# Adapter and expert products of an adaptive FFN kernel, done as packed products of rounded halves and remainders

## The chip, the cores and the metric

The kernel runs on one core of a Trainium2 chip. The metric is the device time of one execution in microseconds. Durations and starts below come from one profiled execution of the kernel before the change.

## What is computed

x has 8 batches of 256 tokens of 1024 features. The first layer quantizes x (8 groups of thresholds, each with its own step and zero point) and puts the result through a mixture of 4 experts of rank 16, of which the router keeps the best 2 by token. The second layer is linear in what comes out of the first: a weight W with a rank-32 adapter chosen by the batch's label, then a kernel K with a rank-32 adapter mixed by a gate, a shared rank-32 adapter and a bias; its result is added to its input.

```python
...
x = x + L0_ffn(L0_cond(x, thresholds, deltas, zero_points), router_w, A, B)
...
base = einsum('bsi,oi->bso', x, W)
low = einsum('bsi,bir->bsr', x, lora_A[labeler_index])
h = base + einsum('bsr,or->bso', low, lora_B_w) * 0.5
...
base_out = matmul(h, kernel) + bias
delta = einsum('bor,btr->bto', B_eff, einsum('bri,bti->btr', A_eff, h))
delta += einsum('or,btr->bto', lora_B_shared, einsum('ri,bti->btr', lora_A_shared, h))
...
x = x + base_out + delta
```

## The kernel before

Because the second layer is linear, the kernel first makes the combined matrix P = I + W'(K + shared adapter), 1024 x 1024, and then the result is x P + bias plus products of low rank. All work is laid out by hand on five engines with semaphores; each engine takes its instructions strictly in the order in which its function writes them, and SyncE's and GpSimd's queues issue the DMAs in order too.

A number a is kept as a rounded half a_hi and a remainder a_lo, both float32r, and a product is taken as a_hi b_hi + a_hi b_lo + a_lo b_hi: three float32r products. Where the factors are plain float32, one product shows in the trace as two records.

The quantization runs beside everything else on ScalarE and VectorE. Its work is cut into 64 groups, `quant(c, g)` for batch c and threshold group g. For one group ScalarE makes `level` (L395) and `val` (L406), and VectorE clips `val` (L598), makes the mask `inside` (L608) and merges (L615); group 1 has two masks, group 0 has the clip alone, and after group 7 VectorE closes the batch (L620). `val`, `level` and `inside` turn over a few buffers, so ScalarE may be only two groups ahead.

**The first part** (to about 202 us) has 16 steps, `for n in range(STEPS)` at each engine. Step n makes one 128 x 512 tile of P. In steps 0 to 7 TensorE first makes tile n of u, the gate's adapters put through W and the label's adapter (L896, 8 float32 products, and L898) in `ubank`; ScalarE copies it to `ust` (L537), which counts `u_made`, and SyncE stores it to `u_dram`. There are two `ust` buffers. TensorE may overwrite `ubank` once `u_made` has counted. Then come the 24 products of the tile (L913, L914, L917), and one k_update (L796). On ScalarE a step is: `weight_hi` of a later tile (L424), the copy of u, `p_out(n - 1)` (L525), the quantization groups of the table `GROUPS`. On VectorE: `k_add` (L647), `weight_lo` (L639), `p_out(n - 1)` (L745), the groups, and the expert ranking where it is due. Steps 1, 6 and 7 among others have one group, steps 2, 4 and 5 two. Between steps 7 and 8 stand `v_product(1)` (L806) and the split of the second half of K (`kp_split`, L431; `kp_lo_part`, L652).

After step 15 TensorE puts the experts' output factor through P (L933 to L935, 48 products of 128 x 512), ScalarE copies that out four times (`bp_out`, L469), and x of batch 0 is split (`x_part`, L455 and L707).

**The second part** runs over 8 batches b of 8 slots j. In a slot TensorE does 12 of the products of x and P (L965 to L967). The slots hold further work at fixed places:

- after slot 4 of each batch, `z_begin(b + 1)`: the adapters with the experts' factor, 64 x 64 (L870), and x with the adapters, 64 x 256 (L874), both plain float32 from `ub` and `xs`; ScalarE copies the first out (`bu_out`, L462);
- near slot 7, `z_end`: one product that adds the experts' share (L881), which ScalarE copies to `zt` (L571), and `close`, the products of `zt` and the adapters' rows `tb` (L942);
- `mid(c)`: the quantized batch c with the experts' A and the router (L848), which waits for VectorE's L620 of that batch. `mid(7)` stands after slot 1 of batch 7. VectorE's ranking of batch c begins with L679 and waits for it;
- the transposes L858 and the output copies L480, 3 slots or more after their tile.

x is loaded in whole batches of 1 MB into one buffer `xs`; batch b + 1 may land when `z_begin(b)` has read it and ScalarE and VectorE have split it.

## Time and profile before

| | us |
|---|---|
| median of 3 runs | 488.16 |
| lowest, highest | 486.01, 490.64 |
| profiled execution, whole | 489.24 |
| its span | 487.5 |
| TensorE busy | 471.8 |
| VectorE busy | 391.4 |
| ScalarE busy | 356.6 |

The span runs from the first to the last instruction; 1.74 us lie outside it. TensorE's busy time rests on modelled ends of pipelined products, so an engine that reads as busy isn't at its peak, and the distance between starts tells more than a record's duration. In timelines the idle time before an instruction stands in brackets with what released it.

### The profile page before, as it was taken

Reading aid. Unit: us, or ns where it says so; the run is one execution under the profiler, and the core shown is the slowest. Engines: PE = TensorE matmul, PEld = TensorE weight load, DVE = VectorE, ACT = ScalarE, POOL = GpSimd, SP = SyncE. Lnnn points to the kernel's source line nnn. Section 1 sums busy time; section 2 is a strip of 40 time slices with the busy share of each in tenths; the row PEclk is TensorE's granted clock in tenths of the full one; section 3 lists DMA queues with packets and bytes.
Section 4 is the critical chain, followed back from the end, with each engine's and each line's share of the span. In section 5 each row is a group of like instructions: output and inputs, shape, how many; then the busy total and the mean of one; then the engine's idle time right before and its main releaser. Section 6 shows DMA issues by size and latency. Waiting matters only on the chain.

```text
span 487.5 us, 5645 instructions
## 1 busy us (share of the span) xinstructions
PE 471.8 (97%) x2200; PEld 365.7 (75%) x2200; DVE 391.4 (80%) x381; ACT 356.6 (73%) x297; POOL 6.8 (1%) x12
## 2 busy tenths in 40 slices
PE   6989999999889999999999999999999999999896
PEld 5963788887648888787777777787787768767774
DVE  3289978789979989939879989798799994999400
ACT  3779987864978398676699599776899697776001
POOL 0000000001000001000000000000000000000000
PEclk9599999999999999999999999999999999999799
DMA  8975542313301527030441316014214013102002
GB/s 281 422 267 178 171 142 73 90 43 98 107 0 37 181 86 204 13 108 1 151 141 44 108 54 200 38 55 130 108 54 152 0 55 129 56 0 86 1 0 87
DMA packets 35500, 50.61 MB, mean 104 GB/s; under 512 B 26610, under 2 KB 26866, under 8 KB 33074
## 3 DMA queue, kind: packets, MB, share of 16 engines
q1 hardware_dynamic: 34322, 41.87, 26.7%
q0 software_dynamic: 1152, 8.39, 4.8%
q8 instruction: 17, 0.28, 0.2%
q14 instruction: 9, 0.07, 0.1%
HBM read 39.51 MB, written 10.49 MB: 103 GB/s over the span
## 4 chain that ended last, share of the span: by engine, by line
PE 76%; DVE 16%; issue 4%; DMA 2%; ACT 1%; SPq 0%; DVEq 0%; ACTq 0%
PE bank L965 10%; PE bank L966 10%; PE bank L967 10%; DVE val L615 7%; PE bank L848 6%; PE bank L942 5%; PE bank L874 5%; PE bank L917 5%; PE bank L913 5%; PE bank L914 4%; PE bank L896 3%; DVE inside L608 3%; PE bank L814 3%; DVE val L598 2%; DMA la<-la_in 2%
## 5 line engine op out<-in xcount | busy, mean ns | idle before, releaser
L406 ACT ACTIVATE val<-level,shift,small 128x2048 f32<-128x2048 int16 x64 | 133.8, 2091 | 16.3 <-DVE val L615 16.2
L615 DVE COPY_PREDICATED val<-inside,val 128x2048 f32<-128x2048 uint8 x56 | 141.3, 2523 | 0.3
L395 ACT ACTIVATE level<-xq,inv 128x2048 int16<-128x2048 f32 x64 | 127.9, 1998 | 2.0 <-DMA xq<-xt_in 1.4
L598 DVE TENSOR_SCALAR val<-val,width,unshift 128x2048 f32<-128x2048 f32 x64 | 86.0, 1347 | 22.7 <-ACT val L406 22.4
L965 PE MATMUL bank<-p_hi,x_hi 128*128 128x512 f32 x256 | 102.5, 401 | 0.0
L966 PE MATMUL bank<-p_lo,x_hi 128*128 128x512 f32 x256 | 100.4, 392 | 0.0
L967 PE MATMUL bank<-p_hi,x_lo 128*128 128x512 f32 x256 | 100.4, 392 | 0.0
L608 DVE TENSOR_SCALAR inside<-absx,thr 128x2048 uint8<-128x2048 f32 x56 | 71.4, 1285 | 7.1 <-ACT absx L387 7.1
L965 PEld LDWEIGHTS bank<-p_hi,x_hi 128*128 128x128 f32 x256 | 48.5, 189 | 17.6 <-issue 8.8
L966 PEld LDWEIGHTS bank<-p_lo,x_hi 128*128 128x128 f32 x256 | 48.4, 189 | 10.5 <-issue 0.5
L967 PEld LDWEIGHTS bank<-p_hi,x_lo 128*128 128x128 f32 x256 | 48.3, 189 | 10.5
L913 PE MATMUL bank<-kp_hi,w_hi 128*128 128x512 f32 x128 | 50.8, 397 | 1.8 <-DVE kp_lo L652 1.8
L917 PE MATMUL bank<-kp_hi,w_lo 128*128 128x512 f32 x128 | 50.4, 393 | 0.0
L914 PE MATMUL bank<-kp_lo,w_hi 128*128 128x512 f32 x128 | 49.9, 390 | 0.0
L848 PEld LDWEIGHTS bank<-ra,val 128*128 128x128 f32 x256 | 31.5, 202 | 3.0 <-DVE val L620 1.7
L848 PE MATMUL bank<-ra,val 128*128 128x68 f32 x256 | 31.5, 284 | 1.3 <-DVE val L620 1.3
L942 PE MATMUL bank<-tb,zt 128*128 128x512 f32 x64 | 32.7, 599 | 0.0
L896 PE MATMUL bank<-aefft,wst 128*128 128x256 f32 x128 | 29.1, 380 | 2.2 <-ACT ust L537 2.2
L874 PE MATMUL bank<-xs,ub 128*64 128x256 f32 x128 | 29.3, 382 | 0.0
L896 PEld LDWEIGHTS bank<-aefft,wst 128*128 128x128 f32 x128 | 24.1, 190 | 6.9 <-issue 3.4
L913 PEld LDWEIGHTS bank<-kp_hi,w_hi 128*128 128x128 f32 x128 | 24.1, 188 | 6.3 <-issue 2.0
L917 PEld LDWEIGHTS bank<-kp_hi,w_lo 128*128 128x128 f32 x128 | 24.0, 188 | 5.2
(91 smaller groups left out, 477.4 us busy)
## 6 DMA issues: line engine op xcount, KB each, us to landing
xq<-xt_in POOLq DMA_DIRECT2D x8, 1024.0 KB, 5.8
xs<-xt_in SPq DMA_DIRECT2D x8, 1024.0 KB, 4.9
out_t<-ost SPq DMA_DIRECT2D x16, 512.0 KB, 3.0
wst<-w_in SPq DMA_DIRECT2D x14, 512.0 KB, 3.6
la<-la_in SPq DMA_DIRECT2D x4, 512.0 KB, 10.4
kst<-k_in SPq DMA_DIRECT2D x4, 512.0 KB, 13.9
lb<-lb_in SPq DMA_DIRECT2D x1, 2048.0 KB, 18.7
kst<-k_in SPq DMA_DIRECT2D x1, 2048.0 KB, 7.9
```

Source lines behind the costliest of these rows:

```text
L395: nc.scalar.activation(level[:, g % 2], xq[:, c % 2], ACT.Copy, scale=inv[:, g:g + 1]).then_inc(levels_made, 1)
L406: nc.scalar.activation(val[:, turn(c, g)], level[:, g % 2], ACT.Relu, bias=shift[:, g:g + 1], scale=par[:, 1, g:g + 1]).then_inc(raised, 1)
L598: nc.vector.tensor_scalar(v, v, width[:, g:g + 1], unshift[:, g:g + 1], ALU.min, ALU.add).then_inc(valued, 1)
L608: nc.vector.tensor_scalar(inside[:, g % 2], absx, thr[:, g - 1:g], None, ALU.is_le).then_inc(masked, 1)
L615: nc.vector.copy_predicated(val[:, acc(c)], inside[:, g % 2], val[:, turn(c, g)]).then_inc(merged, 1)
L848: last = mm(midbank[:, t * RT:(t + 1) * RT], val[:, acc(c), k, t * P:(t + 1) * P], ra[:, k], start=k == 0, stop=k == KT - 1)
L913: mm(obank[n % RING], w_hi[side(n)][:, o], kp_hi[:, o], start=o == 0, stop=False)
L914: mm(obank[n % RING], w_hi[side(n)][:, o], kp_lo[:, o], start=False, stop=False)
L917: last = mm(obank[n % RING], w_lo[side(n)][:, o], kp_hi[:, o], start=False, stop=o == KT - 1)
L965: mm(o, x_hi[:, s, k, at], p_hi[:, h, k], start=False, stop=False)
L966: mm(o, x_hi[:, s, k, at], p_lo[:, h, k], start=False, stop=False)
L967: last = mm(o, x_lo[:, s, k, at], p_hi[:, h, k], start=False, stop=False)
```

## The change

Three products are done in another form.

- The experts' factor is no longer split twice over 128 columns that hold it twice. `betp` holds the remainder in columns 0 to 63 and the rounded half in columns 64 to 127. Its product with P takes two products in place of three (`betp` with p_hi and with p_lo); the two halves of the result lie in different partitions of the bank. ScalarE copies the lower to `tb` (`bp_lo_out`), VectorE adds the upper (`bp_add`), and one copy on ScalarE makes the second `tb` (`bp_copy`).
- The adapters are kept as halves and remainders, 128 columns `packed` (half u, half label adapter, remainder u, remainder label adapter). u is split when it is made: ScalarE writes `ust[:, :, 0]`, VectorE `ust[:, :, 1]` (`u_lo`), and `u_made` is now counted by `u_lo`. There is one `ust` buffer, so ScalarE waits for the store of the tile before. The label adapters of all 5 labels are loaded once (0.66 MB), split (`al_hi` on ScalarE, `al_lo` on VectorE) and stored to `al_dram` (1.3 MB), from where `adapters(b)` loads them.
- `z_begin` is cut in two. `bu_begin(b + 1)` comes after slot 4, 8 products of 128 x 128. ScalarE and VectorE then sum its parts (`bu_out`, `bu_add`). `z_begin(b + 1)` comes after slot 5: 16 float32r products of 128 x 256, `packed` with x_hi and x_lo. It waits for `bu_made` and for both halves of x_lo. ScalarE and VectorE sum its two halves (`z_lo_out`, `z_add`), and `z_end` multiplies all 128 rows of `zt` with `bu`, whose first 64 rows hold the identity.

x is staged in halves of 512 KB (`xs_half`), since z no longer reads `xs`; batch 0's second half has a buffer of its own (`xs_last`). ScalarE splits x after slots 0 and 3 (before: 1 and 3). The ends of batch 0 (`ZEND`, `CLOSE`) move by two slots. Arrays change places in memory.

```diff
-    XAT, ZAT = (1, 3), 4
+    XAT, BUAT, ZAT = (0, 3), 4, 5
...
+            sp.wait_ge(afull, KT // 2)
+            sp.dma_start(al_raw, a["al"].rearrange("l p k r -> p l k r")).then_inc(al_in, 16)
...
+            sp.wait_ge(al_made, 1)
+            sp.dma_start(al_dram.rearrange("l p k h r -> p l (k h r)"),
+                         al_hl.rearrange("p l k h r -> p l (k h r)").bitcast(F32)).then_inc(al_stored, 16)
...
             def u_store(i):
+                sp.wait_ge(u_hi_made, i + 1)
                 sp.wait_ge(u_made, i + 1)
...
             def x_part(c, p):
-                act.wait_ge(xs_in, 16 * (c + 1))
+                if c == 0 and p:
+                    act.wait_ge(xs_last_in, 16)
+                else:
+                    act.wait_ge(xs_in, 16 * (c * XPARTS + p + (c == 0)))
...
+            def z_lo_out(c):
+
+                act.wait_ge(z_read, c + 1)
+                if c >= ZSLOTS:
+                    act.wait_ge(ofull, STEPS + (c - ZSLOTS + 1) * TILES)
+                nc.scalar.activation(zt[0:2 * R, c % ZSLOTS], zbank[2 * R:P, 0:TOK], ACT.Copy).then_inc(z_lo_made, 1)
...
             quant(*ORDER[3])
             v_rows(0)
+            al_hi()
...
                 if n < KT:
                     act.wait_ge(ufull, n + 1)
-                    if n >= 2:
-                        act.wait_ge(u_stored[n % 2], 16 * (n // 2))
-                    nc.scalar.activation(ust[:, n % 2], ubank, ACT.Copy).then_inc(u_made, 1)
+                    if n:
+                        act.wait_ge(u_stored, 16 * n)
+                    nc.scalar.activation(ust[:, :, 0], ubank.rearrange("p (b r) -> p b r", b=BATCH), ACT.Copy).then_inc(u_hi_made, 1)
...
+            def u_lo(n):
+                dve.wait_ge(u_hi_made, n + 1)
+                nc.vector.tensor_tensor(ust[:, :, 1], ubank.rearrange("p (b r) -> p b r", b=BATCH), ust[:, :, 0].bitcast(F32), ALU.subtract).then_inc(u_made, 1)
...
+            def z_add(c):
+
+                dve.wait_ge(z_lo_made, c + 1)
+                z = zt[0:2 * R, c % ZSLOTS]
+                nc.vector.tensor_tensor(z, zbank[0:2 * R, 0:TOK], z, ALU.add).then_inc(z_summed, 1)
+
+            def bu_add(c):
+
+                dve.wait_ge(bu_lo_made, c + 1)
+                part = bu_parts[2 * R:P]
+                nc.vector.tensor_tensor(part, zbank[2 * R:P, TOK:TOK + P], part, ALU.add).then_inc(bu_summed, 1)
+                dve.wait_ge(bu_summed, c + 1)
+                if c >= 2:
+                    dve.wait_ge(zfull, c - 1)
+                nc.vector.tensor_tensor(bu[2 * R:P, c % 2], part[:, 0:2 * R], part[:, 2 * R:4 * R], ALU.add).then_inc(bu_made, 1)
...
             quant(*ORDER[4])
+            al_lo()
...
-                for c, g in GROUPS[n]:
+                for i, (c, g) in enumerate(GROUPS[n]):
                     quant(c, g)
+                    if i == 0 and n < KT:
+                        u_lo(n)
...
+                    if b + 1 < BATCH and j - 1 == BUAT:
+                        bu_add(b + 1)
+                    if b + 1 < BATCH and j - 1 == ZAT:
+                        z_add(b + 1)
                     ranks(slot(b, j))
                     for c, g in GROUPS[slot(b, j)]:
                         quant(c, g)
...
-                    mm(sbank[h], bet_hi[:, k], p_hi[:, h, k], start=o == 0, stop=False)
-                    mm(sbank[h], bet_hi[:, k], p_lo[:, h, k], start=False, stop=False)
-                    last = mm(sbank[h], bet_lo[:, k], p_hi[:, h, k], start=False, stop=o == KT - 1)
+                    mm(sbank[h], betp[:, k], p_hi[:, h, k], start=o == 0, stop=False)
+                    last = mm(sbank[h], betp[:, k], p_lo[:, h, k], start=False, stop=o == KT - 1)
...
+            def z_begin(c):
+
+                t = c % 2
+                packed = ub[:, t].rearrange("p k h a r -> p k (h a r)")
+                pe.wait_ge(bu_made, c + 1)
+                pe.wait_ge(x_lo_made, (c + 1) * XPARTS)
                 for k in range(KT):
-                    last = mm(zbank[0:2 * R, 0:TOK], ub[:, t, k], xs[:, k], start=k == 0, stop=False)
+                    mm(zbank[:, 0:TOK], packed[:, k], x_hi[:, t, k], start=k == 0, stop=False)
+                    last = mm(zbank[:, 0:TOK], packed[:, k], x_lo[:, t, k], start=False, stop=k == KT - 1)
                 last.then_inc(z_read, 1)
```

VectorE's order in steps 0 and 1 of the first part, before (each row: line, operation, output and inputs, shape, the semaphores it waits for):

```order
L598 TENSOR_SCALAR val<-val,width,unshift 128x2048 [waits raised]
L608 TENSOR_SCALAR inside<-absx,thr 128x2048 [waits merged]
L615 COPY_PREDICATED val<-inside,val 128x2048 [waits merged,masked,valued]
L647 TENSOR_TENSOR kst<-bank,kst 128x512 [waits kfull,k2_in]
L639 TENSOR_TENSOR w_lo_100<-wst_102,w_hi_98 128x1024 [waits ofull,w_hi_made]
L745 TENSOR_TENSOR p_lo<-bank,p_hi 128x512 [waits p_hi_made]
```

And the same place with the change, from `al_lo` on:

```order
L766 TENSOR_TENSOR al_hl<-al_raw,al_hl 128x40x32 [waits al_hi_made]
L648 TENSOR_SCALAR val<-val,width,unshift 128x2048 [waits raised]
L658 TENSOR_SCALAR inside<-absx,thr 128x2048 [waits merged]
L665 COPY_PREDICATED val<-inside,val 128x2048 [waits merged,masked,valued]
L762 TENSOR_TENSOR ust<-bank,ust 128x8x32 [waits u_hi_made]
L697 TENSOR_TENSOR kst<-bank,kst 128x512 [waits kfull,k2_in]
L689 TENSOR_TENSOR w_lo_101<-wst_103,w_hi_99 128x1024 [waits ofull,w_hi_made]
L825 TENSOR_TENSOR p_lo<-bank,p_hi 128x512 [waits p_hi_made]
```

L766 and L762 are new; L762, which frees `ubank` for TensorE's next step, stands behind the step's first quantization group.

TensorE's order around z in batch 1, before:

```order
L870 MATMUL bank<-ub,bet 64x64 [waits zt_made,bu_made,bet_in,ub_in1]
L870 MATMUL bank<-ub,bet 64x64 x7
L874 MATMUL bank<-xs,ub 64x256 [waits xs_in]
L874 MATMUL bank<-xs,ub 64x256 x7
L965 MATMUL bank<-p_hi,x_hi 128x512
```

and with the change, where slot 5 and `mid(3)` (L939) come between the two:

```order
L961 MATMUL bank<-ub,betp 128x128 [waits bu_made,zt_made,ub_in0]
L961 MATMUL bank<-ub,betp 128x128 x7
L1064 MATMUL bank<-p_hi,x_hi 128x512
...
L939 MATMUL bank<-ra,val 128x68 [waits mgt_made,ra_in,q_made]
L939 MATMUL bank<-ra,val 128x68 x15
L971 MATMUL bank<-x_hi,ub 128x256 [waits x_lo_made,bu_made]
L972 MATMUL bank<-x_lo,ub 128x256
```

z moved behind slot 5, takes 16 products of 128 weight columns, and waits for two results of VectorE.

VectorE's order at the same place with the change, slots 4 to 6 of a batch; before, the groups followed L707 (here L757) directly:

```order
L757 TENSOR_TENSOR x_lo<-xs,x_hi 128x1024 [waits x_hi_made]
L783 TENSOR_TENSOR bu_parts<-bank,bu_parts 64x128 [waits bu_lo_made]
L787 TENSOR_TENSOR bu<-bu_parts 64x64 [waits zfull,bu_summed]
L648 TENSOR_SCALAR val<-val,width,unshift 128x2048 [waits raised]
L658 TENSOR_SCALAR inside<-absx,thr 128x2048 [waits merged]
L665 COPY_PREDICATED val<-inside,val 128x2048 [waits merged,masked,valued]
L777 TENSOR_TENSOR zt<-bank,zt 64x256 [waits z_lo_made]
```

Three sums are new, and through L783 and L777 VectorE waits for TensorE's two products.

## Rows read from the trace of the kernel before

**Rows 1.** The page: busy time by engine over the whole span.

```profile
PE 471.8 (97%) x2200; PEld 365.7 (75%) x2200; DVE 391.4 (80%) x381; ACT 356.6 (73%) x297; POOL 6.8 (1%) x12
```

**Rows 2.** The chain that ended last, in order of time: start us, us, what.

```profile
141.36 0.62 ACT kp_hi L431
...
142.84 0.47 PE bank L913
...
154.24 3.52 PE bank L848 x32
```

**Rows 3.** VectorE's timeline, steps 0 to 2 and the end of batch 1.

```profile
62.43 0.68 DVE L647 TENSOR_TENSOR kst<-bank,kst 128x512 f32<-128x512 f32 x1
...
64.81 0.69 DVE L745 TENSOR_TENSOR p_lo<-bank,p_hi 128x512 fp32r<-128x512 f32 x1 [0.57 <-ACT p_hi L525]
65.41 1.34 DVE L598 TENSOR_SCALAR val<-val,width,unshift 128x2048 f32<-128x2048 f32 x1
...
70.32 0.67 DVE L647 TENSOR_TENSOR kst<-bank,kst 128x512 f32<-128x512 f32 x1
...
137.16 2.35 DVE L620 SCALAR_TENSOR_TENSOR val<-absx,thr,val 128x2048 f32<-128x2048 f32 x1
```

**Rows 4.** TensorE's timeline, steps 1 and 7: start, us, line, xrecords, [idle before].

```profile
59.80 3.62 PE L896 MATMUL bank<-aefft,wst 128*128 128x256 f32 x16
...
123.82 3.69 PE L896 MATMUL bank<-aefft,wst 128*128 128x256 f32 x16 [2.23 <-ACT ust L537]
```

**Rows 5.** ScalarE's timeline, steps 0 and 1.

```profile
57.47 0.37 ACT L537 ACTIVATE ust<-bank 128x256 f32<-128x256 f32 x1
...
63.90 0.38 ACT L537 ACTIVATE ust<-bank 128x256 f32<-128x256 f32 x1 [1.24 <-PE bank L898]
64.18 0.59 ACT L525 ACTIVATE p_hi<-bank 128x512 fp32r<-128x512 f32 x1
```

**Rows 6.** VectorE's timeline, second part.

```profile
212.50 1.23 DVE L707 TENSOR_TENSOR x_lo<-xs,x_hi 128x1024 fp32r<-128x1024 f32 x1 [4.27 <-ACT x_hi L455]
...
246.66 1.35 DVE L598 TENSOR_SCALAR val<-val,width,unshift 128x2048 f32<-128x2048 f32 x1 [4.55 <-ACT val L406]
...
412.13 0.17 DVE L679 COPY lg<-bank 128x8 f32<-128x8 f32 x1 [5.84 <-PE bank L848]
...
437.64 1.23 DVE L707 TENSOR_TENSOR x_lo<-xs,x_hi 128x1024 fp32r<-128x1024 f32 x1
...
452.43 2.35 DVE L620 SCALAR_TENSOR_TENSOR val<-absx,thr,val 128x2048 f32<-128x2048 f32 x1
```

**Rows 7.** TensorE's timeline, second part.

```profile
201.47 0.39 PE L934 MATMUL bank<-p_lo,bet_hi 128*128 128x512 f32 x1
201.69 0.39 PE L935 MATMUL bank<-p_hi,bet_lo 128*128 128x512 f32 x1
...
433.04 0.97 PE L870 MATMUL bank<-ub,bet 128*64 128x64 f32 x13
...
434.06 3.40 PE L874 MATMUL bank<-xs,ub 128*64 128x256 f32 x15
...
454.84 5.71 PE L848 MATMUL bank<-ra,val 128*128 128x68 f32 x32 [1.29 <-DVE val L620]
```

**Rows 8.** Groups by form: VectorE's smallest product read from PSUM.

```profile
L701 DVE TENSOR_TENSOR mg<-bank,gates 128x128 f32<-128x128 f32 x8 | 2.3, 291 | 0.3
```

**Rows 9.** DMA issues on the page: KB each, median us to landing.

```profile
u_dram<-ust SPq DMA_DIRECT2D x8, 128.0 KB, 4.0
```

**Rows 10.** TensorE's timeline, a short float32r product between long ones.

```profile
54.44 0.22 PE L916 MATMUL bank<-ident 128*128 128x128 f32 x1
54.50 0.44 PE L917 MATMUL bank<-kp_hi,w_lo 128*128 128x512 f32 x1
54.78 0.39 PE L913 MATMUL bank<-kp_hi,w_hi 128*128 128x512 f32 x1
```

**Rows 11.** Windows of 2 us: TensorE busy, granted clock, DMA share, GB/s.

```profile
458.00:460.00 2.00, 2.00 (x11) 0.50 0.00 0
```

More of the change, by code:

```diff
@@ L134, in build @@
     w_bytes = KT * P * 4
-    w_hi = [place(f"w_hi{i}", [P, KT, P], F32R, xs_at, 2 * i * w_bytes)[0] for i in range(2)]
-    w_lo = [place(f"w_lo{i}", [P, KT, P], F32R, xs_at, (2 * i + 1) * w_bytes)[0] for i in range(2)]
-    wst = [place(f"wst{i}", [P, KT, P], F32, at)[0] for i, at in enumerate((ub_at, bet_at))]
+    w_hi = [place(f"w_hi{i}", [P, KT, P], F32R, ub_at, 2 * i * w_bytes)[0] for i in range(2)]
+    w_lo = [place(f"w_lo{i}", [P, KT, P], F32R, ub_at, (2 * i + 1) * w_bytes)[0] for i in range(2)]
+    wst = [place(f"wst{i}", [P, KT, P], F32, at)[0] for i, at in enumerate((xs_at, betp_at))]
     ident_raw, _ = place("ident_raw", [P, P], F32, zt_at)
@@ L251, in former @@
         return {KT: KT - 1, KT + 1: KT - 2}.get(m, m - 2)
-    ZEND = [max(b * KT - 1, OUT_AT[b] - STEPS) for b in range(BATCH)]
-    CLOSE = [max(b * KT + 1, ZEND[b] + 1) for b in range(BATCH)]
+    ZEND = [max(b * KT - 1, OUT_AT[b] - STEPS, 1) for b in range(BATCH)]
+    CLOSE = [max(b * KT + 1, ZEND[b] + 1, 3) for b in range(BATCH)]
     LAG = 3
@@ L349, in _ @@
                     sp.dma_start(bias_raw, a["bias"]).then_inc(bias_in, 16)
[L350 to L354 removed]
+                    sp.wait_ge(vfull, HALVES)
+                    sp.dma_start(bet_raw, a["bet"]).then_inc(bet_in, 16)
+            sp.wait_ge(u_stored, 16 * KT)
+            sp.wait_ge(al_stored, 16)
@@ L369, in _, with rows_store @@
-            xs_load(1)
+            sp.dma_start(xs_last, x_v[0][:, XK:KT]).then_inc(xs_last_in, 16)
+            adapters(0)
+            xs_half(1, 0)
+            adapters(1)
+            def rows_store(b, t):
+                sp.wait_ge(taken, b * TILES + (t + 1) * HALVES)
+                sp.dma_start(out_t[b, t], ost[:, t]).then_inc(out_stored[t], 16)
             for b in range(BATCH):
                 if b + 2 < BATCH:
-                    xs_load(b + 2)
-                for t in range(TT):
-                    sp.wait_ge(taken, b * TILES + (t + 1) * HALVES)
-                    sp.dma_start(out_t[b, t], ost[:, t]).then_inc(out_stored[t], 16)
+                    sp.wait_ge(z_read, b + 1)
+                    adapters(b + 2)
+                if 0 < b < BATCH - 1:
+                    sp.wait_ge(ofull, STEPS + b * TILES)
+                    rows(b + 1)
+                if b + 1 < BATCH:
+                    xs_half(b + 1, 1)
+                if b:
+                    rows_store(b - 1, 1)
@@ L542, in _ @@
                 if n == STEPS - 1:
-                    act.wait_ge(ofull, STEPS - 1)
+                    act.wait_ge(w_lo_made, LOADS - 1)
                     act.wait_ge(bet_in, 16)
-                    nc.scalar.activation(bet_hi, bet, ACT.Copy).then_inc(bet_hi_made, 1)
+                    nc.scalar.activation(betp[:, :, ER:2 * ER], bet_raw, ACT.Copy).then_inc(bet_hi_made, 1)
+                    act.wait_ge(ident_made, 1)
+                    for i in range(2):
+                        last = nc.scalar.activation(bu[0:2 * R, i], ident[0:2 * R, 0:2 * R].bitcast(F32), ACT.Copy)
+                    last.then_inc(eye_made, 1)
                 if n in OUT:
@@ L771, in _ @@
                 for j in range(KT):
+                    if b == 0 and j == 0:
+                        bu_add(0)
+                        for h in range(HALVES):
+                            bp_add(h)
+                        z_add(0)
+                    if b + 1 < BATCH and j - 1 == BUAT:
+                        bu_add(b + 1)
+                    if b + 1 < BATCH and j - 1 == ZAT:
+                        z_add(b + 1)
                     ranks(slot(b, j))
@@ L985, in _ @@
                     gated_turn(TURN[slot(b, j)])
+                if b + 1 < BATCH and j == BUAT:
+                    bu_begin(b + 1)
                 if b + 1 < BATCH and j == ZAT:
```

124 lines of the change are left out of this document (72 added, 52 removed).

## The prediction

> **What bounds the kernel now.** I read the page first: TensorE is busy for 97% of the span and VectorE for 80% [rows 1], so whatever shortens TensorE's stream looks like time won. The chain in order of time says where that holds. In the first part it leaves TensorE between 89 and 142 us and runs over VectorE and ScalarE. At its end ScalarE's first split of K starts at 141.36 and TensorE's step 8 at 142.84 [rows 2]; that split stands behind the close of batch 1 on VectorE, 137.16 + 2.35 us [rows 3]. TensorE's timeline shows the reverse side: it is ahead of the others and waits only 2.23 us before step 7 [rows 4]. It can be ahead because the copy of u (ScalarE, 0.38 us) is all that frees its bank: 63.90 in step 1, right behind the product [rows 5], while VectorE is busy with groups until 70.32 [rows 3].
>
> In the second part the two engines meet once or twice a batch. VectorE waits for ScalarE, which waits for TensorE (4.55 us at 246.66, 5.84 us at 412.13) [rows 6]; before `mid(7)` TensorE waits for VectorE's last batch, closed at 452.43 + 2.35 [rows 6, 7]. What follows it is fixed: 487.5 - 454.8 = 32.7 us. So the end is the time of that close plus 32.7 us, and TensorE's savings count only as far as VectorE follows. Between 414 and 455 us VectorE has hardly a gap.
>
> **First part, the loop through VectorE.** u is now released by `u_lo`, which stands behind the step's first group. Step n's cycle on TensorE was 9.7 us: u's products and the copy's release about 3.9 (59.80 to about 63.7), 24 products of 0.227 (201.47 to 201.69 and their neighbours) and the k_update [rows 4, 7]. The new cycle: product of u 3.9; ScalarE's copy and then p_hi, which is behind it, done 0.9 later (63.90 to 64.77); VectorE's p_lo 0.6; one group 4.9 (65.41 to 70.32); `u_lo` 0.35 [rows 3, 5]. `u_lo` reads 256 columns from PSUM; the nearest rows are 0.29 us for 128 columns and 0.68 for 512, which bound it, and I take 0.35 from start to start [rows 3, 8]. Sum 10.7, with the semaphores 10.8. The wait closes on itself, since p_lo(n - 1) is queued behind u of step n. With group 7 or 1 in front (steps 2 and 3) a group is 6.1 and the cycle 12.0. In steps 4 and 5 the second group falls behind `u_lo`, so VectorE itself is late there, as before.
>
> The start: `al_hi` adds 1.3 us on ScalarE (1280 columns; 1024 take 1.05), of which TensorE sees about 1.0, and `al_lo` 1.4 on VectorE in front of step 0's group, which ended at 62.43 [rows 3]. ScalarE's delay costs VectorE another 0.4. So u of step 0 is released at 62.43 + 1.8 + 0.35 = 64.6, where TensorE started step 1 at 60.0. From there:
>
> - step 2 at 64.6 + 10.8 = 75.4, step 3 at 87.5, step 4 at 99.5 (69.7, 79.4 and 89.2 before);
> - step 5 at 112.8 (step 4 holds `mid(0)`, 3.5 us, and TensorE is the later one): 102.3 before;
> - step 6 at 125.1, step 7 at 139.0: VectorE's groups of steps 4 and 5, the ranking and two waits for ScalarE lie between (112.0 and 124.0 before).
>
> After step 7's start come u 3.9, k_update 0.2, 24 products 5.7, the product with K 7.0 and a transpose 0.45: step 8 at 156.3. VectorE would close batch 1 near 151, so its split is in time. Against 142.84 [rows 2] this is +13.5 us. Steps 8 to 15 are TensorE's own pace and keep it.
>
> Further edits of this part, with one answer: SyncE's queue now holds the store to `al_dram` (1.3 MB), waiting for `al_lo` to 59, ahead of tile 2 of W, which went out at 54.3. It should land by 67, before u of step 1 is done at 68.5, so I cost it at nothing; if it lands later, every us is one us. The store of u took 4.0 us behind half a megabyte of W [rows 9]; it starts now on an empty queue with twice the bytes, and is hidden by the 3.9 us of the next u. Bounds: 0 to 1 us a step, 7 in all. The other end of the sum is that the loop costs only the work it adds to VectorE (1.4 + 7 x 0.35 = 3.9 us). I take 13.5, the place-by-place sum.
>
> **Second part.** The product with P loses 16 products of 0.227: -3.6 us. z in its old form takes 4.35 us a batch: 433.04 to 434.06 for the first and 3.33 for the second, at 0.22 a record [rows 7]. The new form has 8 products of 128 columns and 16 of 256. A float32r product of 128 columns took 0.11 us: L916 and its long neighbour together 0.34, the neighbour alone 0.227 [rows 10]. 256 columns lie between this and 0.227; streaming is half of 512's, so I take 0.115. That gives 0.9 + 1.85 = 2.75, so -1.6 us a batch on TensorE, -12.8 over eight.
>
> The Trainium skill ("TensorE: Matmul & The Clock Gate", LDWEIGHTS) says that a weight load takes a time that goes with the weights' columns, whatever their rows. By it the packed tile loads in 107 ns where 64 columns took 53, which speaks against packing short products. `mid`'s records agree, 0.110 us with 128 weight columns and only 68 moving ones [rows 2]. By the rule with loads hidden z is 16 x 0.107 = 1.7 us; with loads in the open 3.4, and the saving is gone.
>
> VectorE gets three sums a batch. By the 0.29 us row I take 0.45 for the two of `bu_add` and 0.3 for `z_add` [rows 8], 5.3 over seven batches. More weighs that it now waits in order for TensorE's two products, and TensorE for `bu_made`. Followed from meeting to meeting, relative to a first part shifted by 13.5:
>
> - Start: TensorE's first product of batch 0 comes 4.3 us earlier. VectorE stands in `bu_add(0)`, `bp_add` and `z_add(0)` until TensorE has gone through P and z, and starts its groups 2.9 later.
> - The wait of 4.27 us for x at 212.50 [rows 6] goes, since half batches are loaded ahead. By 246.66 both are 3.6 early.
> - In batches 2, 3 and 5 `bu_made` comes after TensorE is at z: x_lo is written late (at 437.64, where the old z began at 434.06) and `bu_add` follows it [rows 6, 7]. TensorE stalls 2 to 3.4 us there, which eats its 1.6. In batches 1, 3 and 6 VectorE waits about 2 us for z.
> - At 412.13 both are 3.7 early; then VectorE alone has 0.8 us more, and in slot 5 of batch 6 it has no group, so `z_add(7)` waits 2.3 us. The last close comes 0.4 early.
>
> The longer wait at `mid(7)` (4 us for 1.29) [rows 7]: `mid` took 5.71 us there where another took 3.52, and the granted clock was 0.50 in 458 to 460, its level of 1.2 GHz [rows 2, 11]. All of it at that level costs 7.0, so +0 to +1.3; I take +0.9.
>
> **Sum** on the profiled execution: 489.24 + 13.5 - 0.4 + 0.9 = 503.2. That execution lies 1.1 us above the median, so 503.0 serves for both.
>
> **Rivals.**
>
> *The clock falls in the first part.* TensorE stands 2 to 4 us before steps 1, 3, 4, 6 and 7. For: after 1.29 us of waiting and `mid` it fell, for about 6.6 us [rows 7, 11]. Against: the 2.23 us before step 7 and dense products after it left it whole [rows 4]. Each fall costs 3.3 us: with two to four, 510 to 516.
>
> *TensorE's savings are kept.* The meetings of the second part cost nothing, because the sums fall into gaps that VectorE has: the close comes 10 us early, as TensorE's -3.6 and five or six times -1.6 allow less `mid(7)`. 503.2 - 9.6 = 493.6.
>
> *Faster after all.* The loop costs only added work, 3.9 us, since VectorE was the late engine at 141 anyway, and TensorE's head start was of no use; with -9.6 behind it, 489.2 + 3.9 - 9.6 = 483.5. It decides if u is released less than 2 us later than before in steps 1 to 3. Against it: the group is queued in front of `u_lo`, 4.9 us of it.
>
> *The new z is no faster.* Products of 256 columns take as long as 512, or loads lie open: z and its partner take 4.5 us, a little above the old. VectorE waits 2 us more per batch where it meets z: 505 to 512, say 508.
>
> **Chances.** Forecast 0.51, clock 0.20, savings kept 0.14, no faster z 0.09, faster after all 0.06. A measurement of this kernel tells 1% (4.9 us) from no change. Savings kept lies at that border, 493.6 against 493.0, so of its 0.14 some 0.05 goes to no change: faster 0.05, same 0.07, slower 0.88. The range reaches from 492 (most of savings kept) to 514 (three falls of the clock).
>
> **What would show it.** Right: TensorE's waits before steps 1 to 7 end with VectorE's L762, about 4, 1, 2, 2, 0, 2 and 4 us; step 8 starts near 156; the products with P take 7.3 us and z's 16 about 1.9; VectorE waits at `z_add` behind TensorE; `mid(7)` waits some 4 us. Wrong: u's release within 2 us of its old time, or step 8 before 150; VectorE's last close more than 5 us off 454.8 + 13.1 = 467.9; a granted clock below 1.00 between 60 and 150 us.

## The result

The changed kernel takes 530.5 us (median of 4 runs, 528.34 to 532.68) where the kernel before takes 488.44 (486.01 to 490.64): ratio 1.0855, interval 1.0806 to 1.0903. That is 42 us slower. The forecast was slower, by 14 us, with 514 as the range's upper end. One execution of a run below, with fills in the changed kernel, came out in a slow state (531.86 us) and is left out of that run's median and ratio.

The page of the changed kernel's profiled execution (span 528.5 us; before 487.5): busy time by engine as in [rows 1], the granted clock in 40 slices, the DMA packets, and the chain's share by engine.

```profile
PE 478.6 (91%) x2120; PEld 376.9 (71%) x2120; DVE 403.5 (76%) x416; ACT 361.3 (68%) x307; POOL 6.7 (1%) x12
...
PEclk8589979899889999999899998899999999999789
...
DMA packets 54348, 55.46 MB, mean 105 GB/s; under 512 B 43154, under 2 KB 44050, under 8 KB 52946
...
DVE 38%; PE 31%; ACT 13%; issue 11%; DMA 6%; SPq 0%; ACTq 0%; DVEq 0%
```

TensorE has 80 instructions fewer and yet more busy time, since parts of it run at the lower clock. VectorE has 35 more and 12 us more work. The chain that sets the end now runs over VectorE for 38% of the span, more than over any other engine.

The first part, from TensorE's timeline: u's products of steps 0 to 7 and the first product of step 8 (start, us, records, [idle before]). Before, these were [rows 4] and the 142.84 of [rows 2].

```profile
52.85 3.72 PE L996 MATMUL bank<-aefft,wst 128*128 128x256 f32 x16
66.26 6.34 PE L996 MATMUL bank<-aefft,wst 128*128 128x256 f32 x16 [3.43 <-DVE ust L762]
80.25 3.69 PE L996 MATMUL bank<-aefft,wst 128*128 128x256 f32 x16 [1.38 <-DVE ust L762]
92.69 5.09 PE L996 MATMUL bank<-aefft,wst 128*128 128x256 f32 x16 [2.48 <-DVE ust L762]
106.31 3.69 PE L996 MATMUL bank<-aefft,wst 128*128 128x256 f32 x16 [2.26 <-DVE ust L762]
119.53 3.62 PE L996 MATMUL bank<-aefft,wst 128*128 128x256 f32 x16
132.31 5.38 PE L996 MATMUL bank<-aefft,wst 128*128 128x256 f32 x16 [2.99 <-DVE ust L762]
146.10 5.38 PE L996 MATMUL bank<-aefft,wst 128*128 128x256 f32 x16 [2.25 <-DVE ust L762]
...
169.13 0.47 PE L1013 MATMUL bank<-kp_hi,w_hi 128*128 128x512 f32 x1 [2.13 <-DVE kp_lo L702]
```

Six waits end with `u_lo` (L762), as forecast. In four of the six steps the products behind the wait take 5.1 to 6.3 us instead of 3.7. Between step 7 and step 8 lie 23 us, where 19 were before. What happened there stands on three engines: SyncE's queue, ScalarE and VectorE.

```profile
152.02 0.33 SPq L354 DMA_DIRECT2D wst<-w_in  x1
152.44 0.39 SPq L346 DMA_DIRECT2D u_dram<-ust  x1
```

```profile
157.17 0.38 ACT L582 ACTIVATE ust<-bank 128x256 fp32r<-128x256 f32 x1 [13.94 <-DMA u_dram<-ust]
157.45 0.59 ACT L570 ACTIVATE p_hi<-bank 128x512 fp32r<-128x512 f32 x1
```

```profile
158.08 0.69 DVE L825 TENSOR_TENSOR p_lo<-bank,p_hi 128x512 fp32r<-128x512 f32 x1 [10.53 <-ACT p_hi L570]
...
163.16 2.35 DVE L670 SCALAR_TENSOR_TENSOR val<-absx,thr,val 128x2048 f32<-128x2048 f32 x1
...
168.29 4.31 DVE L702 TENSOR_TENSOR kp_lo<-kst,kp_hi 128x512 fp32r<-128x512 f32 x7 [2.44 <-ACT kp_hi L455]
```

The store of u of step 6 was ready at 146 (VectorE wrote its remainders at 145.55). It left at 152.44, because in SyncE's queue it stands behind a load of W that waits for u's products of step 7, the last of which ends at 151.9. ScalarE may not overwrite `ust` before that store has landed, so it stood 13.94 us and took p_hi and VectorE with it. Not all of this is the store's: u of step 7 itself was there only at 151.9, so the late store is the last 5.2 us. Batch 1 closes at 163.16 instead of 137.16 [rows 3].

The second part: what TensorE, ScalarE and VectorE waited for from 168 to 492 us (us in total, times, longest).

```profile
PE bank L971 <- DVE bu L787: 13.8, 6, 3.4
```

```profile
ACT zt L496 <- PE bank L972: 23.8, 8, 5.3
ACT x_hi L482 <- DMA xs<-xt_in: 13.0, 6, 3.4
```

```profile
DVE zt L777 <- ACT zt L496: 13.1, 5, 3.6
DVE val L648 <- ACT val L430: 9.6, 5, 3.4
DVE bu_parts L783 <- ACT bu_parts L489: 5.2, 2, 3.6
```

Three engines wait for each other around z: TensorE for `bu_add` on VectorE, ScalarE for z, VectorE for ScalarE.

ScalarE's waits for x are of another kind. Six times, once a batch from 284 us on, it stands 1.3 to 3.4 us before it can split a half of x. There is one buffer `xs` for a half, so the second half's load leaves only when VectorE has split the first; before, with whole batches, ScalarE had two such waits in this part (6.2 us), both ahead of 212 us.

```profile
321.52 1.06 ACT L482 ACTIVATE x_hi<-xs 128x1024 fp32r<-128x1024 f32 x1 [3.01 <-DMA xs<-xt_in]
```

The second part is measured on VectorE, from the first `kp_lo` of K's second half to the start of the last batch's closing instruction: 142.0 to 452.4 before (310.4 us), 168.3 to 491.9 after (323.6 us), so +13. With +26.3 before it, the last close is 39.4 us late; `mid(7)` now waits 4.47 us and takes 6.57 [rows 7].

```profile
494.27 6.57 PE L939 MATMUL bank<-ra,val 128*128 128x68 f32 x32 [4.47 <-DVE val L670]
```

### The profile page after: what moved, and what is told of

It is laid out like the page before. It is cut to its first block, busy times and chain, and to the rows that moved or that the text cites. A ratio compares the mean times of both kernels' runs of the same rounds, so it can differ in the third digit from the quotient of the medians.

```text
span 528.5 us, 5563 instructions
## 1 busy us (share of the span) xinstructions
PE 478.6 (91%) x2120; PEld 376.9 (71%) x2120; DVE 403.5 (76%) x416; ACT 361.3 (68%) x307; POOL 6.7 (1%) x12
## 4 chain that ended last, share of the span: by engine, by line
DVE 38%; PE 31%; ACT 13%; issue 11%; DMA 6%; SPq 0%; ACTq 0%; DVEq 0%
DVE val L665 17%; DVE inside L658 8%; DVE val L648 6%; ACT val L430 4%; ACT level L419 4%; PE bank L996 3%; PE bank L939 3%; PE bank L1013 3%; PE bank L1017 3%; PE bank L1014 3%; PE bank L905 3%; PE bank L1064 2%; PE bank L1065 2%; PE bank L1066 2%; DMA u_dram<-ust 2%
## 5 line engine op out<-in xcount | busy, mean ns | idle before, releaser
L1065 PE MATMUL bank<-p_lo,x_hi 128*128 128x512 f32 x256 | 101.7, 397 | 0.0
L1066 PE MATMUL bank<-p_hi,x_lo 128*128 128x512 f32 x256 | 101.5, 396 | 0.0
L1064 PEld LDWEIGHTS bank<-p_hi,x_hi 128*128 128x128 f32 x256 | 49.5, 194 | 13.8 <-issue 4.7
L996 PE MATMUL bank<-aefft,wst 128*128 128x256 f32 x128 | 36.9, 453 | 14.8 <-DVE ust L762 14.8
L996 PEld LDWEIGHTS bank<-aefft,wst 128*128 128x128 f32 x128 | 29.0, 231 | 23.2 <-issue 18.0
L939 PEld LDWEIGHTS bank<-ra,val 128*128 128x128 f32 x256 | 32.2, 206 | 8.9 <-DVE val L670 8.3
L939 PE MATMUL bank<-ra,val 128*128 128x68 f32 x256 | 32.7, 290 | 6.2 <-DVE val L670 6.1
L971 PE MATMUL bank<-x_hi,ub 128*128 128x256 f32 x64 | 19.5, 333 | 13.8 <-DVE bu L787 13.8
```

Source lines behind the costliest of these rows:

```text
L939: last = mm(midbank[:, t * RT:(t + 1) * RT], val[:, acc(c), k, t * P:(t + 1) * P], ra[:, k], start=k == 0, stop=k == KT - 1)
L996: mm(ubank, wst[n % 2][:, o], aefft[:, o], start=o == 0, stop=False)
L1064: mm(o, x_hi[:, s, k, at], p_hi[:, h, k], start=False, stop=False)
L1065: mm(o, x_hi[:, s, k, at], p_lo[:, h, k], start=False, stop=False)
L1066: last = mm(o, x_lo[:, s, k, at], p_hi[:, h, k], start=False, stop=False)
```

## Experiments on the first part

**`u_lo` ahead of the groups on VectorE.**

```
 for n in range(STEPS):
+    if n < KT: u_lo(n)
     for c, g in GROUPS[n]: quant(c, g)
-        u_lo(n) behind the first group
```

> The changed kernel with u_lo moved ahead of the step's first quantization group on VectorE; nothing else. Loop theory (u is released late because u_lo is queued behind a group): TensorE's waits before steps 1 to 7 (14.8 us) all but go, the clock falls of these steps go with them, step 8 starts about 20 us earlier (about 149 for 169.6), the store of u(6) still holds ScalarE in step 7, and the whole takes about 511. Rival (VectorE's load, not its order, paces the first part): u_lo only changes places with a group, step 8 moves by less than 4 us, the whole stays above 525.

Measured: 516.1 us, ratio 1.0565 (1.0507 to 1.0624); step 8 at 157.89. So 10 to 11 us of the first part hung on that one place in VectorE's order. That is half of the 20 us that I expected: `u_lo` still kept TensorE waiting before steps 2, 6 and 7 (8.9 us), with slow products behind it, and ScalarE still stood 8.4 us before a copy of u, until the late store had landed.

A word on such starts: the executions come to step 0 at different times, from 50.32 to 52.85 us with the same instructions ahead of it (49.97 before the change). Counted from step 0's start, step 8 comes after 92.9 us before and 116.3 in the changed kernel, 106.6 here, 102.0 with both mends, 112.7 with the fills and 97.8 with u copied, all below.

**The store of u ahead of the load of W in SyncE's queue.**

```
 for m in range(2, LOADS):
+    u_store(m - 2)
     sp.wait_ge(w_hi_made, ...); sp.wait_ge(w_lo_made, ...); sp.wait_ge(ufull, ...)
     sp.dma_start(wst[...], w_v[...])
-    u_store(m - 2)
```

> The changed kernel with SyncE's store of u tile m-2 put ahead of the waits for W's tile m, so that the store of u(6) isn't queued behind the wait for step 7's u. Queue theory: ScalarE's copy of u in step 7 starts at TensorE's 151.9 in place of 157.1, the 13.9 us wait for the store shrinks to 8 or so, the whole gains 5 us: 525. Rival (the store is late by its own length, 4.6 us): no change, 530.

Measured: 528.2 us, ratio 1.0846 (1.0775 to 1.0918), no difference from the changed kernel. ScalarE's wait for the store was gone, but the loads of W now stood behind a wait for `u_lo`, and came late. ScalarE's waits over the span:

```profile
ACT w_hi L448 <- DMA wst<-w_in: 16.9, 4, 8.2
```

**Both.**

> Both of the above. If the first part's loss is the release of u and the store's place, step 8 starts at 144 to 146 (before the change 142.8) and the whole takes about 506; what is left over 488 then belongs to the second part. If the adapters' split and its 1.3 MB store cost by themselves, step 8 stays at 150 or later.

Measured: 512.8 us, ratio 1.0512 (1.0472 to 1.0553); step 8 at 154.57. This is above the 506 that I expected, and step 8 later than the 144 to 146: TensorE still waits for `u_lo` before steps 2, 4, 6 and 7 (10.3 us), in steps 6 and 7 for 3.4 and 4.0 us. With u released early the store's new place costs little: ScalarE waits for W once, 6.4 us (4.3 with the first mend alone). The gain over the first mend alone is some 3 us by the medians, but the two intervals overlap.

**Idle time before u filled with products of no use.** 18 products of 128 columns in front of each wait for u's bank, in the changed kernel.

```
+    for _ in range(18): mm(obank[n % RING][:, 0:P], ones, ones, start=True, stop=True)
     pe.wait_ge(u_made, i)
```

> The changed kernel with 18 products of 128 columns on TensorE, which nothing reads, ahead of each wait for u in steps 1 to 7 (about 2 us each), into the bank of the next tile. Clock theory (the waits themselves are covered, but each lets the granted clock fall, which made u's products 6.3, 5.1, 5.4 and 5.4 us in place of 3.7): the granted clock stays 1.00 between 60 and 150 us, u's products take 3.7 in every step, and the whole gains 5 to 7 us: 524. If the clock's falls are hidden under VectorE's pace, the clock stays up and the time stays 530.

Measured: 523.4 us, ratio 1.0759 (1.0702 to 1.0817). u's products all take 3.7 us, the granted clock has no slice under its neighbours between 40 and 300 us, and step 8 starts at 165.21 for 169.13:

```profile
PEclk8599999999999999999999998999999998999589
```

Adding work to TensorE made the kernel about 5 us faster by the ratios, whose intervals just touch; its three executions, 523.1 to 525.9 us, all lie below the changed kernel's 528.3 to 532.7. So the falls of the clock are a cost of their own, here some 4 us at step 8.

**u's bank released by a plain copy, as before**, and with it two `ust` buffers, as before.

```
-    nc.scalar.activation(ust[:, :, 0], ubank, ACT.Copy).then_inc(u_hi_made, 1)
+    nc.scalar.activation(u_raw[:, n % 2], ubank, ACT.Copy).then_inc(u_copied, 1)
     p_out(n - 1)
+    nc.scalar.activation(ust[:, n % 2, :, 0], u_raw[:, n % 2], ACT.Copy).then_inc(u_hi_made, 1)
 ...
-    pe.wait_ge(u_made, i)
+    pe.wait_ge(u_copied, i)
```

> The changed kernel with u's bank released as before the change: ScalarE copies it whole to SBUF (256 columns), TensorE waits for that copy alone, and the halves and remainders are made from the copy, behind p_hi on ScalarE and behind the first group on VectorE, into two buffers in turn. Store queue unchanged. Theory A (the loop over u_lo, the clock that falls in its waits, and the one late store are the loss of the first part, beyond VectorE's added work of 1.5 + 8 x 0.41 = 4.8 us): TensorE does not wait for VectorE before steps 1 to 6, u's products stay at 3.7 us, step 8 starts at 146 to 150 instead of 169.1, time 505 to 511. Theory B (VectorE's order or the loads of W are late in any case): step 8 at 153 or later, time 513 or more.

Measured: 509.9 us, ratio 1.0423 (1.0351 to 1.0494); step 8 at 148.95, 20 us earlier than in the changed kernel. TensorE waits for VectorE nowhere in the first part, and only twice for ScalarE, before steps 6 and 7. The queue of stores is unchanged, and with two buffers no wait on ScalarE ends with a store of u. What stays of the first part is 6 us. The second part takes 323.7 us, as in the changed kernel.

**The adapter table's split alone, in the kernel before.**

```
+    sp.dma_start(al_raw, a["al"])       # and its store to al_dram, which nothing reads
+    al_hi()                             # ScalarE
+    al_lo()                             # VectorE
```

> The kernel before, with only the split of the adapter table added: its load, the rounded half on ScalarE (1.3 us), the remainder on VectorE (1.5 us), and its store to a table in DRAM, which nothing reads (the adapters are loaded as before). Theory A (its cost is VectorE's and ScalarE's time in front of step 0, and the store is hidden): step 8 is 1 to 2 us later than 142.84, time 489 to 491. Theory B (the store stands in SyncE's queue ahead of a tile of W and that delays steps 1 or 2): step 8 is 4 us later or more, time 493 or more. Theory C (all of it lies beside other work): within 1 us.

Measured: 491.1 us, ratio 1.0041 (1.0001 to 1.0081). In the profiled execution `kp_lo` begins at 147.07, 5 us later than before, and its span is 492.5, above the median of its runs. The interval reaches from nothing to 4 us; the median is theory A's, while step 8, at 147.91 for 142.84, is as late as theory B had it. Theory B's mechanism isn't there, though: from step 0 to steps 1 and 2 TensorE takes what it took before (9.8 and 19.6 us). It began step 0 at 52.55 (49.97 before) and waited for ScalarE's copy 1.25 us before step 6 and 3.29 before step 7, where u's products then took 5.4 us for 3.7. The second part is 310.4 us, to the tenth what it was.

## Experiments on the second part

**z's meeting alone, in the kernel before.** z stands one slot later and waits for bu and for x_lo, with the old products.

```
-    XAT, ZAT = (1, 3), 4
+    XAT, ZAT = (1, 3), 5
 ...
-    pe.wait_ge(xs_in, 16 * (c + 1))
+    pe.wait_ge(bu_made, c + 1); pe.wait_ge(x_lo_made, (c + 1) * XPARTS)
```

> The kernel before, with only the meeting of the second part changed: z's product with x stands one slot later and waits for bu and for both halves of x_lo, as in the changed kernel; products, sums and loads stay the old ones. In the changed kernel the stretch from the second kp_lo to the last close takes 323.6 us where it took 310.4 before. Theory A (the meeting is most of these 13 us, because TensorE now stands in front of z and the others behind it): the stretch takes 316 us or more here, the time is 493 or more. Theory B (the added sums on VectorE and the clock are most of it): the stretch stays within 3 us of 310.4, the time within 4 us of 488.

Measured: 492.5 us, ratio 1.0101 (1.0062 to 1.0140); the stretch is 318.7 us for 310.4. By the stretch this is theory A, by the time half of it, as `mid(7)` no longer waits for VectorE there and the profiled execution is the slowest of ten (495.2 us). VectorE's waits for `val` grew from 16.7 to 22.4 us in the stretch, ScalarE's for z and bu from 27.3 to 38.2. Between the two bounds that I had set, the run shows that the meeting costs something without any new work. How much of the 13 us in the changed kernel, with its shorter z, it does not show.

**VectorE's sums for bu and z left out** (in the version with both mends).

```
-    DVE: bu_add(b + 1), z_add(b + 1)
+    ACT: bu <- zbank[ER:2 * ER], zt <- zbank[0:2 * R]
```

> The version with both mends of the first part (512.8 us), without VectorE's sums for bu and z: ScalarE copies the upper half of each product straight into bu and zt, so the remainders' share of these two is left out; every TensorE product stays, and TensorE still waits at z for bu and x_lo. VectorE has 0.93 us a batch less, 7.4 in all, and does not wait for z (11.7 us in 4 waits) nor for bu (3.4) any more. Theory A (the sums with the waits in VectorE's order are the loss of the second part): the stretch from kp_lo to the last close falls from 322.9 to 311 or less, time 500 to 503. Theory B (ScalarE's stand behind z and the late halves of x are it): it falls by the 7 us of work at most, and VectorE's waits for val grow instead; time 505 to 510.

Measured: 500.9 us, ratio 1.0299 (1.0218 to 1.0379) against 1.0512 for the same kernel with them. The stretch falls from 322.9 to 312.1 us: 10.8, of which VectorE's busy time explains 6.1 (284.7 to 278.6). The other 5 us are waits that went with the sums.

**Fills before u and before z** (same base).

> The version with both mends of the first part (512.8 us), with 12 short products of no use ahead of each wait for u's bank and 18 ahead of each wait before z, into a bank that the next tile clears. They take 1.3 and 2 us of waits that are there anyway (z's waits are 16.0 us in 6). Theory A (a good part of what is left is the clock, at 1.2 GHz behind these waits): u's products stay at 3.7 us, granted clock 1.00 in nearly all slices, first part 3 to 5 us shorter, the second 3 to 4: time 505 to 508. Theory B (VectorE and ScalarE set the second part whatever TensorE's clock): first part shorter by 2 to 4, second by less than 1: 509 to 511. If the fills come in the way, it is slower than 512.8.

Measured: 514.9 us, ratio 1.0551 (1.0475 to 1.0626): no gain over 1.0512 (1.0472 to 1.0553). The stretch is 324.4 us for 322.9. Both theories were wrong by a few us. In the first part the fills did their work on TensorE, whose products of u all take 3.7 us, and yet `kp_lo` begins only 1.2 us earlier (151.91 for 153.11): in this version the clock is worth little there. In the second part they shortened TensorE's waits before z from 16.0 us in 6 to 5.1 in 4, but the granted clock over the stretch rose only from 0.979 to 0.984, so the run does not show what the clock costs there.

**Another order around z** (same base). bu and its sums one slot earlier, ScalarE's copy and VectorE's sum of z one slot later than z's products.

```
-    XAT, BUAT, ZAT = (0, 3), 4, 5
+    XAT, BUAT, ZAT = (0, 3), 3, 5
 ...
-    if j == ZAT: z_lo_out(b + 1)          # ScalarE
+    if j == ZAT + 1: z_lo_out(b + 1)
 ...
-    if j - 1 == ZAT: z_add(b + 1)         # VectorE
+    if j - 2 == ZAT: z_add(b + 1)
```

> The version with both mends of the first part (512.8 us), with another order in the second: bu's product and its sums one slot earlier, ScalarE's copy of z's lower half and VectorE's sum one slot later than z's product. The work is the same. Without the sums the stretch from kp_lo to the last close was 312.1 us, with them 322.9, of which 7.4 us are VectorE's work. Theory A (the other 3.4 us are waiting in order, and order cures it): the stretch falls to 319 to 320, TensorE's waits before z (16.0 us in 6) fall by half, time 508 to 510. Theory B (the waits only move): stretch within 1 us of 322.9, time 512 to 514.

Measured: 502.7 us, ratio 1.0287 (1.0217 to 1.0357), 10 us better than its base at equal work. The stretch is 316.0 us with VectorE's busy time at 285.0, as it was. ScalarE's wait for z fell from 26.1 us to

```profile
ACT zt L496 <- PE bank L972: 7.2, 5, 1.9
```

and VectorE's waits for the copy (11.7 us in 4 before, from batch 1 on) are gone. This is more than my theory A allowed; I had counted only what VectorE waited at z itself; the likely rest, which no run takes apart, is what ScalarE, held in its own order, withheld from the groups behind.

## Experiments on both parts

**u copied, and the other order.**

> Both repairs together: u's bank released by a copy, and the second part in the other order. Sum of the two theories A: 502 to 507, above 488 in any case, since VectorE's added work (4.8 us in the first part, 8.7 in the second) stays. If the kernel with both comes below 496, the added work on VectorE is not the loss that is left.

Measured: 497.3 us, ratio 1.0162 (1.0091 to 1.0232), better than the 502 to 507 that I wrote down. Of the changed kernel's 8.5% there are 1.6% left. TensorE's waits from 50 to 470 us:

```profile
PE bank L983 <- DVE x_lo L769: 13.1, 5, 3.7
PE bank L1008 <- ACT u_raw L587: 5.8, 2, 3.6
```

**The same without VectorE's sums.**

> The kernel with both repairs (497.3 us), without VectorE's sums for bu and z: ScalarE copies the upper half of each product straight to its place, so the remainders' share of these two is left out. VectorE has 0.93 us a batch less, 7.4 in all; with the repaired order it waited only 1.4 us for z and 4.9 for bu. Theory A (what is left over the kernel before is VectorE's added work): the stretch from kp_lo to the last close falls from 315.6 us by 6 or more, to the 310 of the kernel before, time 489 to 492. Theory B (the clock and TensorE's waits before z for x_lo, 15 us in 6, are what is left): it falls by less than 3, time 494 to 497.

Measured: 488.5 us, ratio 0.9990 (0.9952 to 1.0028): the time of the kernel before. The stretch is 305.2 us, 10.4 less, with 7.0 less of VectorE's work. In the first part this version is still 6.5 us behind the kernel before, and makes it good in the second, where TensorE's shorter products do count once VectorE has hardly more to do than before (277.7 us busy in the stretch, 276.9 before). ScalarE's waits for x are still there (10.2 us in 6).

**The same with the sums, and with fills before steps 6 and 7 and before z.**

> The kernel with both repairs (497.3 us), with 14 short products of no use ahead of the waits before steps 6 and 7 and before each z. u's product of step 7 took 6.7 us there for 3.7, and products behind z's waits run at 1.2 GHz for some us. Theory A (VectorE's work): step 8 up to 3 us earlier on TensorE, the last close within 2 us, time 495 to 498. Theory B (clock): granted clock 1.00 in nearly all slices, last close 4 us or more earlier, time 491 to 493.

Measured: 495.5 us, ratio 1.0154 (1.0079 to 1.0229), not to be told from 1.0162. The granted clock is 0.989 between 150 and 460 us here (0.978 without the fills), and the last close comes 1.5 us earlier. Half of the lost clock came back for no gain clear of noise, and leaving the sums out gave back all that was left. So what is left over the kernel before goes with VectorE's sums, and the clock's part in it is small; the other half of its loss was not taken away.

**The product with P alone, in the kernel before.** Two packed products for three, with the two sums on VectorE.

```
-    mm(sbank[h], bet_hi[:, k], p_hi[:, h, k], ...)
-    mm(sbank[h], bet_hi[:, k], p_lo[:, h, k], ...)
-    mm(sbank[h], bet_lo[:, k], p_hi[:, h, k], ...)
+    mm(sbank[h], betp[:, k], p_hi[:, h, k], ...)
+    mm(sbank[h], betp[:, k], p_lo[:, h, k], ...)
```

> The kernel before with only the product with P in two packed products instead of three, with its two sums on VectorE. TensorE does 16 products of 0.227 us less, 3.6 us; VectorE 1.3 us more. Theory A (what VectorE closes sets the end, so TensorE's saving counts only as far as VectorE follows): the products take 7.3 us instead of 10.9, the time stays within 2 us of 488. Theory B (a saving there reaches the end): 484 to 485.

Measured: 484.2 us, ratio 0.9925 (0.9888 to 0.9963): faster than both kernels. Theory B holds. In its trace the closes from the fourth on come 3 us early (449.46 for the last, 452.43 before), and `mid(7)` waits 1.26 us as it did. This is the piece of the change worth keeping: 16 products of 512 columns gone, for 1.3 us of sums once in the kernel and not once a batch.

## Why the prediction was right in direction and wrong in size

*What bounds the kernel; the end follows VectorE's last close.* Right. The last close moved by 39.4 us and the span by 41.0. Of the 27.4 us between the forecast 503.2 and the profiled execution's 530.6, 12.8 are there at step 8, 13.6 come in the stretch up to the last close, and 1 behind it.

*The loop through `u_lo`.* Right as a mechanism and near in size. Forecast starts of steps 1 to 7 were 64.6, 75.4, 87.5, 99.5, 112.8, 125.1 and 139.0; measured 66.26, 80.25, 92.69, 106.31, 119.53, 132.31 and 146.10. About 2 us of the difference are there at step 1, and the execution had begun step 0 late, at 52.85 (51.19 and 51.32 in two of the experiments). By step 2 it is 4.9 us late; there the slow products and the store of step 1 come in, see below. The run with `u_lo` moved shows that the place of the group in front of it was the cause.

*"The clock falls in the first part" as a rival with 0.20.* This is the first step that failed. I put 0 in the sum because one wait of 2.23 us had left the clock whole [rows 4]. Here the granted clock was 0.53 in 66 to 72 us and 0.72 in the stretches behind the waits of 2.48, 2.99 and 2.25 us:

```profile
66.00:72.00 6.00, 5.74 (x14) 0.53 0.97 309
80.00:84.00 4.00, 3.75 (x18) 1.00 0.29 66
92.00:98.00 6.00, 5.31 (x21) 0.72 0.19 44
132.00:138.00 6.00, 5.69 (x21) 0.72 0.46 152
146.00:152.00 6.00, 5.89 (x21) 0.72 0.00 0
```

(window, its length, TensorE busy, granted clock, DMA share, GB/s). The four slow products of u took 22.2 us for 14.8. With six waits of the kind that I had forecast myself, one instance without a fall was thin evidence against one with it; the fills show some 4 us at step 8 to be the price in the changed kernel.

*"It starts now on an empty queue with twice the bytes, and is hidden by the 3.9 us of the next u."* This is the second. I costed the store's transfer at its old length and left out its place in the queue. In the changed kernel the copy waits for the store of the step just before, and for one store SyncE's queue puts a wait for the very next u ahead of it. Of ScalarE's 13.94 us there, the last 5.2 are the store's. Step 8 fell another 5.7 us behind the forecast (7.1 late at step 7, 12.8 at step 8). Of these, 1.7 are u's slow products of step 7, for whose end the load of W and so the store waited; 3.9 are TensorE's two waits for VectorE, 1.81 us before L897 and 2.13 before step 8. Nor was the transfer hidden in step 1. The store of u(0) left at 66.20 and took 7.0 us to land, with the DMA engines 0.97 busy, and ScalarE stood before the copy of step 1:

```profile
73.30 0.38 ACT L582 ACTIVATE ust<-bank 128x256 fp32r<-128x256 f32 x1 [3.77 <-DMA u_dram<-ust]
```

With the fills, u's products of step 1 took 3.7 us and this wait 2.54; step 2 still started 6.8 us after that copy, where it was 6.9 here, and 13.8 after step 1 for 14.0. My bound of 7 us in all held the size, but I took 0. That `al_dram`'s store would be hidden was nearly right: the load of W behind it (queued at 61.99) made ScalarE wait 4.0 us once.

*The product with P.* Right: its 32 products run from 218.96 to 226.40 us, 7.4 us for the forecast 7.3, and the run of it alone shows that the gain reaches the end.

*z's products.* Right. 16 products from 229.31 to the next at 231.32 are 2.0 us for the forecast 1.85, at 0.12 us each:

```profile
229.54 0.28 PE L972 MATMUL bank<-x_lo,ub 128*128 128x256 f32 x1
229.65 0.28 PE L971 MATMUL bank<-x_hi,ub 128*128 128x256 f32 x1
229.77 0.28 PE L972 MATMUL bank<-x_lo,ub 128*128 128x256 f32 x1
```

The estimate worked out from the Trainium skill ("TensorE: Matmul & The Clock Gate", LDWEIGHTS) is 1.7 us with the weight loads hidden and 3.4 with them in the open. This trace, with 2.0, is near the first.

*"The last close comes 0.4 early."* This is the third, and with 13 us the largest. Four terms of it:

- The sums cost 0.93 us a batch (0.42 for `z_add`, 0.51 for `bu_add`) where I took 0.75, and `bp_add` 1.3 us that stood in no term. VectorE's busy time in the stretch rose by 7.9 us.
- I let the engines drift apart from meeting to meeting and made up the gains. Near the close of batch 3 VectorE was to be 3.6 us early; it was 0.6 late (288.43 for 261.54, after `kp_lo` was 26.3 late). Without batch 0's, I had three stalls of TensorE before z, of 2 to 3.4 us each, and it had five, 11.9 us in all; for VectorE I had four waits for z, some 8 us, and it had four, 11.7 us.
- I followed VectorE and TensorE and left ScalarE out. It copies z's lower half in the same slot in which TensorE computes z, so it stood 23.8 us behind z. What VectorE needs from it next, `val` for the next group, stands behind that in ScalarE's order. The other order without any change of work took 7 us from the stretch and 10 from the time.
- "Half batches are loaded ahead" took away the wait of 4.27 us at 212.50 and put six in its place, ScalarE's 13.0 us for x. No run takes them away, so their share of the 13 us is not known; the version without VectorE's sums still has 10.2 us of them at the time of the kernel before.

*`mid(7)`.* Right: it waits 4.47 us for the forecast 4, and takes 6.57 where 5.71 + 0.9 was forecast.

*The rival "faster after all"* has a slip in its sum: a close 10 us early and `mid(7)`'s +0.9 give 484.0, where I wrote 483.5. It changes nothing.

*The ledger*, from the ratios at 488.4 us, in the order in which the pieces were taken away: 42 us in all. Releasing u's bank by a copy gives back 21 (loop, clock and late store together), the other order around z 13 more, VectorE's sums of bu and z, with the waits that hang on them, the last 8. In that last version the 6 us that stay in the first part are made good by TensorE's savings in the second.

Open: how the 6 us that stay in the first part divide. The table's split is somewhere between 0 and 4 us of the whole time, and u's remainders are 8 x 0.41 = 3.3 us of VectorE's time; a run without the remainders was not made.

## What to carry to other kernels

Before work moves from an engine that is ahead to one that sets the end, price it on the second engine: here the 15 us or so that P and z save on TensorE at the full clock were bought with 12 us more on VectorE, and waits in order cost more than either. Whoever releases a buffer should stand at the front of its own queue; a copy of 0.4 us that frees the bank at once is cheaper than a sum that is only one instruction but behind 5 us of others. For each new wait, list what is queued behind it on *every* engine, the DMA issuer included, and ask which of these the wait's own releaser depends on.

## What the runs showed of the hardware

A wait on TensorE costs more than its length. Behind waits of 2.25 to 3.43 us the granted clock fell in most cases and not in all: 2.26 us before step 4 left u's products at 3.69 us, 2.25 us before step 7 made them 5.38. Products of 256 columns in z ran 0.21 us apart at the lower level (328.93 to 329.14 us, granted clock 0.50) and 0.12 at the upper one. Products of no use in such gaps gave 5 us in the changed kernel, where TensorE was what the others waited for, and nothing clear of noise in the two versions that release u early, though the second part's clock came back there only in part. There are 18,848 DMA packets more, 16,544 of them under 512 B; ScalarE's waits for loads and stores grew as well (4.0 us for W and 3.8 for a store in the first part, 13.0 for x in the second), but no run shows how much of it is the packets and how much the order of the issues.
